# SyncE issues two context loads behind the stacking of a chunk, where one of them stood in front of it

## What is computed

```python
x = x + tanh(g_xattn) * xattn(layernorm(x), ctx, mask)
x = x + tanh(g_ffn) * ffn(layernorm(x))

# xattn: q from x, k and v from ctx
scores = clip(einsum('bhsd,bhtd->bhst', q, k) / 4, -50, 50)
scores = clip(where(attend, scores, -10000), -50, 50)
ctx = einsum('bhst,bhtd->bhsd', softmax(scores), v)
delta = residual_scale * (ctx @ Wo.T + bo)      # then a layernorm of delta

# ffn: weights quantized to three values, activations to 8 bits
h = silu(bitlinear(x, w1)) * bitlinear(x, w2)
return bitlinear(h, w3)
```

## Time and profile before

| | |
|---|---|
| median of three timed runs | 1332.48 us (1331.07 to 1334.24) |
| profiled execution | 1329.38 us, span 1327.6 us, granted clock 0.987 |
| TensorE matmul busy | 1282.6 us, 97% |
| VectorE busy | 1069.2 us, 81% |
| ScalarE busy | 947.9 us, 71% |
| GpSimd busy | 394.4 us, 30% |
| SyncE's queue | 202.06 MB, 62.5% of the 16 transfer engines' span |

### The profile page before, as it was taken

The page is one execution under the profiler, slowest core; times in us unless marked ns, Lnnn a source line. Parts: engine busy times, 40 slices in busy tenths (PEclk is TensorE's granted clock), DMA queues, the critical chain, the costliest instruction groups (busy, mean ns, idle before and its releaser), DMA issues.

```text
span 1327.6 us, 47302 instructions
## 1 busy us (share of the span) xinstructions
PE 1282.6 (97%) x19802; PEld 1177.7 (89%) x19802; DVE 1069.2 (81%) x2085; ACT 947.9 (71%) x1561; POOL 394.4 (30%) x695
## 2 busy tenths in 40 slices
PE   5999999999999999999999999999999999999983
PEld 4988998999999999999999999999999999999972
DVE  5777888779888789886888886888778889778864
ACT  4766777677777767776767776777777877777761
POOL 4322333222333231322331323331233331133310
PEclk9999999999999999999999999999999999999986
DMA  8867777677777777777676768766777776777630
GB/s 238 204 161 180 168 171 183 168 173 182 170 170 184 174 175 174 169 170 197 171 171 168 178 160 203 174 168 160 175 188 176 180 170 163 179 182 175 149 78 11
DMA packets 146187, 225.38 MB, mean 170 GB/s; under 512 B 29674, under 2 KB 139310, under 8 KB 145966
## 3 DMA queue, kind: packets, MB, share of 16 engines
q1 hardware_dynamic: 132312, 202.06, 62.5%
q0 software_dynamic: 12288, 19.69, 6.4%
q10 hardware_dynamic: 1366, 0.53, 0.2%
HBM read 57.27 MB, written 3.28 MB: 46 GB/s over the span
## 4 chain that ended last, share of the span: by engine, by line
PE 89%; SPq 4%; DVE 3%; DMA 2%; issue 1%; ACT 1%; POOL 0%; DVEq 0%; POOLq 0%; ACTq 0%
PE sc L1252 23%; PE pvb L1272 20%; PE cb L1307 19%; PE cb L1293 18%; SPq L331 4%; PE mb L1367 2%; PE mb L1335 2%; PE mb L1345 2%; DMA k_st<-k_lo 1%; PE mb L1382 1%; DVE zt L880 1%; PE mb L1374 1%; PE mb L1328 0%; DMA c_in<-in_ctxT 0%; DVE k_lo L793 0%
## 5 line engine op out<-in xcount | busy, mean ns | idle before, releaser
L572 ACT ACTIVATE e_sb<-sc 121x800 f32<-121x800 f32 (+1 forms) x768 | 644.7, 844 | 187.2 <-PE sc L1252 176.5
L1252 PE MATMUL sc<-q_st,k_st 96*121 96x200 f32 (+1 forms) x3072 | 469.4, 275 | 8.3 <-DMA k_st<-k_lo 5.2
L1252 PEld LDWEIGHTS sc<-q_st,k_st 96*121 96x121 f32 (+1 forms) x3072 | 411.1, 185 | 40.0 <-issue 9.0
L802 DVE TENSOR_SCALAR e_sb<-e_sb,hi_b 121x1600 f32<-121x1600 f32 (+1 forms) x384 | 404.2, 1056 | 12.3 <-ACT e_sb L572 12.1
L1272 PE MATMUL pvb<-e_sb,v_sb 121*32 121x100 f32 x12288 | 286.5, 251 | 0.0
L1272 PEld LDWEIGHTS pvb<-e_sb,v_sb 121*32 121x32 f32 x12288 | 265.2, 110 | 23.5 <-issue 20.4
L793 DVE SCALAR_TENSOR_TENSOR k_lo<-cb,bk_c,k_hi 128x484 fp32r<-128x484 f32 (+1 forms) x192 | 134.5, 701 | 132.8 <-ACT k_hi L584 132.5
L492 POOL DMA_DIRECT2D q_st<-bd_hi x256 | 157.5, 619 | 269.2 <-DVE bd_lo L848 263.8
L1307 PE MATMUL cb<-wv_hi,c_hi 128*121 128x256 f32 (+1 forms) x768 | 221.7, 289 | 2.4 <-DVE k_lo L793 1.3
L1307 PE MATMUL cb<-wv_hi,c_lo 128*121 128x256 f32 (+1 forms) x768 | 215.6, 281 | 0.0
L1307 PE MATMUL cb<-wv_lo,c_hi 128*121 128x256 f32 (+1 forms) x768 | 215.5, 281 | 0.0
(11 more groups left out here) (160 smaller groups left out, 1351.1 us busy)
## 6 DMA issues: line engine op xcount, KB each, us to landing
k_st<-k_hi SPq DMA_DIRECT2D x512, 121.0 KB, 3.0
c_in<-in_ctxT SPq DMA_DIRECT2D x64, 484.0 KB, 3.9
k_st<-k_lo SPq DMA_DIRECT2D x256, 121.0 KB, 3.2
k_st<-k_hi SPq DMA_DIRECT2D x256, 119.0 KB, 3.3
c_in<-in_ctxT SPq DMA_DIRECT2D x32, 476.0 KB, 3.8
k_st<-k_lo SPq DMA_DIRECT2D x128, 119.0 KB, 3.0
q_st<-bd_hi POOLq DMA_DIRECT2D x256, 50.0 KB, 3.3
q_st<-bd_lo POOLq DMA_DIRECT2D x128, 50.0 KB, 3.2
```

The costliest lines, as they stand in the source:

```text
L572: nc.scalar.activation(e_sb[e_slot(b, n)][0:TL[n], k * SW:(k + 1) * SW].rearrange("p (o c) -> p o c", o=2), sc[q % NSC][0:TL[n], :, 0:2 * PW],
L802: V.tensor_scalar(e, e, E_LO, hi_b[b.par][0:TL[n], n:n + 1], ALU.max, ALU.min).then_inc(clip_done, 1)
L1252: last = T_.matmul(sc[q % NSC][0:TL[n], e // 2, (e % 2) * PW:(e % 2 + 1) * PW], k_st[st_slot(b, n // TPC)][:, pr // NQ, pr % NQ, t0:t0 + T ...
```

## The change

In `batch` of SyncE, the stacking of chunk 0 of the next batch is moved ahead of the load of chunk 0 of the batch after next. The load keeps its wait. Both loads now stand one behind the other.

```diff
                 stack_k(b, 2)
+                if nxt:
+                    stack_k(b.plus(1), 0)
                 if nxt2:
                     sp.wait_ge(split_done, SPLIT.after(b.plus(1), "lo1"))
                     load_c(b.plus(2), 0)
-                if nxt:
-                    stack_k(b.plus(1), 0)
-                if nxt2:
                     sp.wait_ge(split_done, SPLIT.after(b.plus(1), "lo2"))
                     load_c(b.plus(2), 1)
```

## The result

The changed kernel takes 1338.6 us (median of 20 runs, 1332.95 to 1343.55), the kernel before, run on the same chips, 1333.31 us (20 runs, 1328.75 to 1337.68). The ratio is 1.0039, with a 95% interval of 1.0025 to 1.0053: slower, by some 5 us. The forecast was no change, 1332.5 us with a range up to 1338.5; both are missed, the upper end of the range by 0.1 us.

What follows compares the result with a forecast made beforehand. TensorE, busy 97% of the span, was taken as the bound, so only its waits count. The four steps summed 0 + 0 + 0 + 0: no change, 1332.5 us as a median, range 1328.5 to 1338.5.

Steps and rivals of the forecast that it cites:

- Steps 1 and 2: SyncE's stackings of chunks 0 and 1: waits for the scores hide the loads' issue; 0, at most 7.3 us gained.
- Step 3: VectorE's cast c_hi: load 1.9 us late in batches without feed-forward group, covered by 2.9 us idle; 0, at most 13.
- Step 4: Transfer engines before and during the stacking of chunk 1: 496 KB more fit at 218 GB/s; cost 0.
- The step's upper bound: Transfer engines: 496 KB wholly on top, 2.3 us; seven batches lack 0.2 to 1.1 us, about 5 us together.
- the slower cases: SyncE's stacking of chunk 1 pushed back (+5 us), or VectorE waiting for the load (+13 or +36 us); chance 0.17.
- The 5 us of the first: SyncE's stacking of chunk 1 pushed back by the second load: +5 us, 1337.5 us; chance 0.12.

Runs made afterwards that it cites:

- the first batch alone: Against the kernel before: the changed order in the first batch only, the order of before in the other 29; ratio 1.0023 (1.0004 to 1.0042).
- one load less: Against the changed kernel: the load of chunk 1 that batch 0 issues goes out behind the next stacking; ratio 1.0006 to the kernel before.

## Why the prediction was wrong, point by point

*Steps 1 and 2* held: SyncE's stackings of chunks 0 and 1 are still started by the scores, and TensorE's waits for stacked keys stayed at 7.6 us. Their reading of the earlier trace rows was not clean, since the longest of those waits was for a query copy.

*Step 3*, VectorE's cast, held in its mechanism and its cover. The two loads are in a row, and in a batch with a group the cast comes in time. In the short batch around 630 us it is 1.47 us late, less than the 1.9 of the step; the next k_lo follows without the idle time that it had the earlier trace rows, and 2.18 us of idle time are left before pT. VectorE's timeline of the changed kernel:

```profile
629.85 0.67 DVE L762 CAST c_hi<-c_in 128x968 fp32r<-128x968 f32 x1 [1.47 <-DMA c_in<-in_ctxT]
630.43 0.71 DVE L792 SCALAR_TENSOR_TENSOR k_lo<-cb,bk_c,k_hi 128x476 fp32r<-128x476 f32 x1
...
634.29 0.42 DVE L868 TENSOR_SCALAR pT<-pvb,submask 128x200 f32<-128x200 f32 x1 [2.18 <-PE pvb L1271]
```

The first load's landing, taken as 5.2 us, was 3.7 to 6.8, half of them 4.3 or less; the nine waits, two of them in the prologue as before, make 6.5 us in all, and the length of the 28 batches shows that they reach hardly anyone.

*Step 4* failed: "what shares the transfer engines with it". The price of the loads beside the stacking copies was right, 0 within the 0.6 us of 28 batches. The step asked only for the copies of SyncE's own queue, and it took the stretch from 659.9 to 671.5 for all thirty. GpSimd's query copies use the same engines (by the page of the kernel before 19.69 MB in all, 6.4% of the 16 engines' span), TensorE waits for them at the first scores of a batch, and in the first batch they are issued late enough to stand behind the loads. There the term is 2.75 us more of waiting (3.74 against 0.99) and 1.6 us of lower clock in place of 0. The trace of the kernel before had the sign: waits of 0.99 and 1.39 us for just these copies at the first scores of batches 1 and 2. (The step's upper bound was also counted high: by its own margin of 1.3 us against 2.3 needed, no batch can lack more than 1.0 us, not 1.1.)

*The rivals*: the slower cases had 0.17, and both had the wrong place, the stacking of chunk 1 and VectorE's cast. The 5 us of the first came out as the size by accident.

## What to carry to other kernels

A transfer that is moved in one queue must be held against every queue that feeds the same consumer: list what each engine has yet to issue at the new place, batch by batch at the start, and not only in the batch that repeats. A cost worked out on the steady batch says nothing of the first two, in which a slower producer can stand on the other side of the moved transfer. And where a wait is for two transfers, the row may name neither ("issue" at 71.30), or the wrong one (stacked keys at 107.29): what tells is when each landed. A wait can also be removed by order alone: the two loads kept apart (0.9967 and 0.9968), or held back once (0.9984), beat both kernels.

## What the runs showed that was not expected

A query copy of 50 KB issued on GpSimd's queue behind 484 KB loads of SyncE's queue landed about when they did: in the changed kernel at 71.2, 0.5 us after the second load; in the one with the first batch alone at 71.4 against 70.8. A copy issued just ahead of the loads was late too: with one load less, the copy of 104.89 took 5.9 us beside loads of 105.5 and 106.1. How the transfer engines divide their time between the two queues was not measured.

Behind waits of 2.29, 3.26, 3.30 and 3.74 us at the first scores of batch 1 TensorE's granted clock stood at half for 3.4 us, and each time batch 1, less the wait at the first scores of batch 2, was 1.6 us longer (39.2 us against 37.6); behind the waits of 0.99 to 1.71 us at the same place it stayed at 1.00. At the first scores of batch 2 the length of the wait does not sort the cases: the clock fell behind 1.74, 2.05, 2.75, 2.81 and 2.95 us, and stayed at 1.00 behind 1.92 and 3.05.
